# Cross attention and routed experts: sums in their own buffer, the output normalised first, 71 slots

## The chip, the core and the metric

The kernel runs on one core of a Trainium2 chip. The metric is the device time of one execution in microseconds (us). The core has five engines: PE (TensorE, matmuls and transposes), DVE (VectorE), ACT (ScalarE), POOL (GpSimd) and SP (SyncE, whose queue issues most of the DMAs). Each runs its own list of instructions in order and waits on semaphores. Matmuls write into PSUM, of which this kernel uses eight banks: A0 to A3 and B0 to B3.

## What is computed

x is 4096 tokens (16 sequences of 256) of 512 values. The core of the reference:

```python
x = x + xattn(layernorm(x), ctx, ctx, ...)      # 16 heads of 32
#   score = einsum('bshd,bsgd->bshg', Q, K): for one token, its 16 heads against its 16 heads
#   weight = softmax(score); attn = einsum('bshg,bsgd->bshd', weight, V); attn @ Wo.T + bo
x = x + ffn(layernorm(x), ...)
#   logits = z @ gate.T, softmax over 8 experts, the best 2 kept with their weights
#   routed: silu(z @ g) * (z @ u) @ down per picked expert, F = 352
#   shared: the same with 704 hidden values for all tokens
```

Attention is thus within a token, between its heads, and each token goes to two of eight experts.

## The kernel before

**Block loop.** The tokens go through in 16 blocks of 256, two halves of 128 each (SUB = 2). A pass i of the loop (`body(i, ...)`, written out once for each engine) works on three blocks at the same time: scores, softmax and attending of block i; the projections K, Q and V of block i + 1 ("ahead"), with the statistics and the normalising of x of block i + 2 ("ahead2"); and behind them block i - 1 ("behind"): its attended sums are projected by Wo, added to x, normalised to z, and z is transposed, split into two fp16 parts and multiplied with the router's weights. `FULL_PASS` (lines 67 to 78) is PE's order in a pass and says which bank each step fills: X (transposes of the normalised x), S (scores), K, Q, O (projection by Wo), T (transposes of the spread softmax weights), V, Z (transposes of z), L (router logits), P (attend), LT, M0. A step waits until all earlier fills of its bank have been read (`wait_free`); L and Z0 share B2.

**Who does what.** In a pass ACT copies the attended sums out of PSUM (`attended_out`, 24 small copies, DVE does 8 more), then X, K and Q, the exponentials, the T banks (`weights_out`), and the Z banks (`z_out`). DVE reduces the scores, splits operands into a high and a low part, does the softmax, the statistics, `normalise_x`, `add_attended`, `normalise_out`, `values_out`, the largest value of the context block after next (`weigh_context`, `spread_context`), and the low part of z (`z_low`), which is the last reader of a Z bank. POOL spreads the softmax weights into block diagonal form (line 1820, four instructions for each half), finds 1/std (`inverse_std`, lines 1776 and 1777) and splits the context block (`split_context`: a cast, line 1796, and a subtraction, line 373). SP moves K and Q between layouts through 24 DMAs, loads x, the residual and the context, and stores x1, z, the parts of z and the values.

`at_raw`, the buffer of the attended sums, is another view of `z` (line 224). So its writers, ACT and DVE, wait for `z_stored`, the store of the last z to DRAM (lines 1095 and 1414).

**Around it.** Behind the loop an epilogue runs the last block's output between the first steps of the shared experts. Then come the router's ranking, 12 blocks of the shared experts, and the slots: the two picks of each token are sorted by expert into tiles of 128 rows, each tile of one expert. `SLOTS` = 72 of them run (line 34: 64 + 8), in pairs, two buffers each; a slot gathers its 128 rows of z, transposes them, multiplies by gate and up, and by down, and stores 128 rows. Last come the other four blocks of the shared experts together with the weighted sum of each token's two rows.

Of the kernel before, what the change touches and what calls it, by code (L numbers as in the profile page):

```python
# [15 lines left out]
P = 128  # L16
# [5 lines left out]
SUB = 2  # L22
# [11 lines left out]
SLOTS = T * TOPK // P + E  # L34
# [95 lines left out]
def build(nc, x, ctx_t, wq_t, bq, wk_t, bk, wv_t, bv, wo_t, bo, wgate_t, wgu_t, wdn_t, wsgu_t, wsdn_t, out):  # L130
    with ExitStack() as whole:
# [92 lines left out]
        at_raw = z[:, :, :].rearrange("p s (c t) -> p (s c) t", t=BT)  # L224
# [219 lines left out]
        def _(sp):  # L444
# [180 lines left out]
            with sp.Fori(0, SLOTS // 2) as k:  # L625
                for b in range(2):
                    j = k * 2 + b
                    sp.wait_ge(d_out, j + 1)
                    settle(sp)
                    sp.dma_start(y_d[bass.ds(j * P, P), :], y_sb[:, b, :]).then_inc(y_stored[b], 16)  # L630
# [20 lines left out]
        def _(pe):  # L651
# [358 lines left out]
            with pe.Fori(1, SLOTS // 2 - 1) as k:  # L1010
# [6 lines left out]
            j = SLOTS - 2  # L1017
            open_expert(j, 0)
            turn_rows(j + 1, 1, SLOTS // 2 - 1)
            close_expert(j - 1, 1)  # L1020
            turn_act(j, 0)
            open_expert(j + 1, 1)
            close_expert(j, 0)
            turn_act(j + 1, 1)
            close_expert(j + 1, 1)
# [6 lines left out]
        def _(act):  # L1032
# [29 lines left out]

            def z_out(i):
                if not (isinstance(i, int) and i == 1):
                    act.wait_ge(zt_stored, (i - 1) * 16)
                for s in range(SUB):
                    wait_full(act, f"Z{s}", i)
                    turned = bank_ap(f"Z{s}").rearrange("p (c t) -> p c t", c=KC)
                    copy(z_t[:, :, s * P:(s + 1) * P], turned).then_inc(z_turned, 1)
                    nc.scalar.activation(z_parts[:, HI, :, s * P:(s + 1) * P], turned, ACT.Copy, scale=2.0 ** Z_EXP).then_inc(zt_high, 1)  # L1070
# [22 lines left out]
            def attended_out(i):  # L1093
                wait_full(act, "P0", i - 1)
                act.wait_ge(z_stored, i * 16)
# [4 lines left out]
            def body(i, behind, ahead):  # L1100
# [14 lines left out]
                weights_out(1, i)  # L1115
                if isinstance(i, int) and i == NB - 1:
                    act.wait_ge(ws_scaled, 1)
                    shared_high(range(KC))
# [28 lines left out]
            z_out(NB)  # L1147

# [86 lines left out]
            with act.Fori(2, SLOTS // 2 - 1) as k:  # L1235
                for b in range(2):
                    step(k * 2 + b, b, k)
            for j in range(SLOTS - 2, SLOTS):
                step(j, j % 2, j // 2)
            rows_out(SLOTS - 1, 1, SLOTS // 2 - 1)  # L1240
# [29 lines left out]
        def _(dve):  # L1270
# [120 lines left out]
            def z_low(i):  # L1391
                for s in range(SUB):
                    dve.wait_ge(zt_high, (i - 1) * SUB + (s + 1))
# [566 lines left out]
```

## Time and profile before

| | us |
|---|---|
| median of 3 runs | 1666.06 (1652.44 to 1668.23) |
| the profiled execution | 1661.5 |
| its span, first to last instruction | 1659.8 |
| PE busy | 1478.1 (89%) |
| DVE busy | 848.2 (51%) |
| ACT busy | 630.0 (38%) |
| POOL busy | 494.2 (30%) |
| mean granted TensorE clock | 0.954 of full |

The chain of work that ended last consists of PE to 49%, DVE to 15%, SP's queue to 10%, DMA to 8% (5% are the store of z) and ACT to 7%. Busy shares are means over stages: DVE is busy for seven to eight tenths of the block loop (until about 690 us) and for one tenth of the slots (1013 to 1523 us). A row's "idle before" is the time its engine stood still ahead of it, with what ended that.

### The profile page before, as it was taken

What the parts mean: (1) busy time and instruction counts of PE and PEld (TensorE: products, weight loads), DVE (VectorE), ACT (ScalarE), POOL (GpSimd) and SP (SyncE); (2) the same over time, 40 slices, a digit from 0 to 9 for tenths busy, and PEclk for the clock granted to TensorE, in tenths of its full rate; (3) what the DMA queues carried; (4) which work ended last, traced back from release to release, by engine and by line L of the source; (5) the groups of instructions that cost most, each with busy time, mean ns of one, the idle gap of its engine ahead of it and who ended that gap; (6) DMA issues with size and microseconds to landing.
All of it is one profiled execution on the core that took longest, in us unless ns stands there. A gap on an engine that the chain in (4) does not pass through costs nothing.

```text
span 1659.8 us, 32612 instructions
## 1 busy us (share of the span) xinstructions
PE 1478.1 (89%) x10194; PEld 1092.1 (66%) x10211; DVE 848.2 (51%) x1797; ACT 630.0 (38%) x1481; POOL 494.2 (30%) x607
## 2 busy tenths in 40 slices
PE   5489999999999998668979997999999999999786
PEld 5488887788888886446657774666666666666443
DVE  6577788777877887558525532111111111111565
ACT  5255555555555654422114421222222222222111
POOL 4244444433333333102663001111111111111564
PEclk9799999999999998779989998999999999999888
DMA  5346566665665657192344252222222222222897
GB/s 184 78 107 143 144 146 150 155 158 166 158 143 143 143 116 229 56 339 90 52 64 78 76 196 95 76 75 76 75 75 76 74 76 75 76 75 93 283 332 249
DMA packets 258247, 215.61 MB, mean 130 GB/s; under 512 B 182688, under 2 KB 190953, under 8 KB 257850
## 3 DMA queue, kind: packets, MB, share of 16 engines
q1 hardware_dynamic: 240196, 170.63, 37.1%
q0 software_dynamic: 12960, 35.73, 7.6%
q10 hardware_dynamic: 5046, 8.66, 1.6%
q8 instruction: 26, 0.43, 0.1%
q14 instruction: 19, 0.16, 0.0%
HBM read 120.52 MB, written 69.28 MB: 114 GB/s over the span
## 4 chain that ended last, share of the span: by engine, by line
PE 49%; DVE 15%; SPq 10%; DMA 8%; issue 8%; ACT 7%; POOL 1%; another core or an unknown queue 1%; DVEq 0%; ACTq 0%; POOLq 0%
PE psum_a L653 23%; PE psum_b L653 22%; SPq L455 9%; DMA z_rows<-z 5%; ACT z L1034 5%; DVE sc L1364 3%; PE psum_b L961 2%; PE psum_b L983 1%; DMA wgu_in<-expert_rows,pos_ix 1%; DVE d_m L1591 1%; DVE gate_act L1566 1%; DVE k_parts L1307 1%; DVE stats L1292 1%; ACT wgu L1184 1%
## 5 line engine op out<-in xcount | busy, mean ns | idle before, releaser
L653 PE MATMUL psum_a<-wgu,zg_t 128*128 x1728 | 271.4, 314 | 1.7 <-DVE zg_t L1713 1.7
L1718 DVE SCALAR_TENSOR_TENSOR silu<-psum_a,w_scale,silu 128x352 f32<-128x352 f32 x72 | 42.0, 584 | 408.8 <-ACT silu L1217 408.8
L1820 POOL TENSOR_TENSOR spread<-pr,own 128x512 f32<-128x512 f32 x128 | 139.0, 1117 | 357.2 <-DVE pr L1379 352.2
L1894 POOL DMA_INDIRECT zg<-z_rows,gather_ix x72 | 68.1, 946 | 530.5 <-DVE gather_ix L1709 522.8
L653 PEld LDWEIGHTS psum_a<-wgu,zg_t 128*128 128x128 f16 x1728 | 169.6, 98 | 85.5 <-issue 2.4
L653 PE MATMUL psum_b<-wdn,act_t 128*128 (+1 forms) x432 | 197.6, 593 | 0.9 <-ACT act_t L1034 0.9
L653 PE MATMUL psum_b<-wsdn,sh_t 128*128 128x512 f16 (+1 forms) x576 | 150.1, 416 | 43.1 <-DVE sh_t L1572 31.1
L653 PE MATMUL psum_a<-zt_in,wsgu 128*128 128x256 f16 x1536 | 173.5, 275 | 6.0 <-DVE wsgu L1409 5.3
L653 PEld LDWEIGHTS psum_a<-zt_in,wsgu 128*128 128x128 f16 x1536 | 150.5, 99 | 31.5 <-issue 11.6
L653 PEld LDWEIGHTS psum_b<-wsdn,sh_t 128*128 128x128 f16 (+1 forms) x576 | 57.1, 105 | 130.5 <-issue 42.5
L1034 ACT ACTIVATE z<-psum_a 32x128 f32<-32x128 f32 x384 | 102.7, 267 | 54.7 <-DMA z_rows<-z 48.7
L653 PEld LDWEIGHTS psum_b<-wdn,act_t 128*128 128x128 f32 (+1 forms) x432 | 76.6, 191 | 70.0 <-issue 70.0
L1217 ACT ACTIVATE silu<-psum_a,w_scale 128x352 f32<-128x352 f32 x72 | 39.8, 553 | 206.2 <-PE psum_a L653 206.2
L653 PE MATMUL psum_b<-cx_t,wk 128*128 128x256 f32 x768 | 109.2, 298 | 5.6 <-DVE wk L373 5.6
L653 PE MATMUL psum_a<-k_st,q_st 104*128 104x128 f16 x512 | 78.3, 294 | 40.2 <-DMA q_st<-q_parts 24.7
L653 PEld LDWEIGHTS psum_b<-cx_t,wk 128*128 128x128 f32 x768 | 101.7, 203 | 6.1 <-DVE wk L373 6.0
L1161 ACT ACTIVATE gate_act<-psum_a,ws_scale 128x256 f32<-128x256 f32 x64 | 30.0, 471 | 198.5 <-PE psum_a L653 168.5
L653 PE MATMUL psum_b<-xn_t,wq 128*128 128x256 f32 x768 | 104.7, 290 | 0.0
L653 PE MATMUL psum_b<-wo,at_t 128*128 128x512 f32 x384 | 100.5, 416 | 1.1 <-DVE at_t L373 1.1
L1034 ACT ACTIVATE y_sb<-psum_b 128x512 f32<-128x512 f32 x72 | 43.0, 597 | 148.7 <-PE psum_b L653 148.7
L653 PEld LDWEIGHTS psum_b<-xn_t,wq 128*128 128x128 f32 x768 | 97.3, 195 | 0.1
L653 PE MATMUL psum_b<-wv,cx_t 128*128 128x512 f32 x384 | 93.2, 399 | 2.2 <-ACT q_parts L1042 2.2
(229 smaller groups left out, 2385.0 us busy)
## 6 DMA issues: line engine op xcount, KB each, us to landing
expert_rows<-y_sb SPq DMA_DIRECT2D x72, 256.0 KB, 2.9
k_st<-k_parts SPq DMA_DIRECT2D x192, 64.0 KB, 2.1
q_st<-q_parts SPq DMA_DIRECT2D x192, 64.0 KB, 2.2
wgu_in<-in_wgu_t SPq DMA_DIRECT2D x8, 1408.0 KB, 15.6
x_sb<-in_x SPq DMA_DIRECT2D x16, 512.0 KB, 3.5
cx_in<-in_ctx_t SPq DMA_DIRECT2D x16, 512.0 KB, 6.5
x_res<-in_x SPq DMA_DIRECT2D x16, 512.0 KB, 5.2
value_rows<-heads SPq DMA_DIRECT2D x16, 512.0 KB, 6.0
```

Source lines behind the costliest of these rows:

```text
L455: sp.dma_start(dst[HD * n:HD * (n + 1), :, HD * l:HD * (l + 1), :].rearrange("p j m g -> p j (m g)"), parts[HD * l:HD * (l + 1), part].rea ...
L653: return nc.tensor.matmul(o, l, r, start=start, stop=stop)
L961: last = nc.tensor.transpose(t_bank[:, kc * P:(kc + 1) * P], zg[:, b, kc * P:(kc + 1) * P], ident[:, :])
L983: last = nc.tensor.transpose(a_bank[0:fn, f * P:(f + 1) * P], silu[:, b, f0:f0 + fn], ident[:, :])
L1034: return nc.scalar.activation(o, i_, ACT.Copy)
L1161: nc.scalar.activation(gate_act[at:at + fn, f % GB, :], sh_bank(f)[0:fn, 0:BT], ACT.Silu, scale=ws_scale[0:fn, 3:4]).then_inc(silu_ready, 1)
L1184: act.activation(wgu[:, bass.ds(e * UNIT + c * 2 * F, 4 * F)], wgu_in[:, bass.ds(e + 1, 1), c:c + 2, :].rearrange("p o c n -> p (o c n)"), ...
L1217: nc.scalar.activation(silu[:, b, :], psum_a[:, 2 * b * BANK:2 * b * BANK + F], ACT.Silu, scale=w_scale[:, 3:4]).then_inc(g_silu, 1)
L1364: ins = V.tensor_reduce(out=sc[:, s, u * UG:(u + 1) * UG, :], in_=bank_ap(step).rearrange("p (r g t) -> p r g t", r=UG, t=GT), axis=X, op= ...
L1718: V.scalar_tensor_tensor(out=silu[:, b, :], in0=psum_a[:, (2 * b + 1) * BANK:(2 * b + 1) * BANK + F], scalar=w_scale[:, 3:4], in1=silu[:, ...
L1820: G.tensor_tensor(spread[:, u * UG:(u + 1) * UG, :].rearrange("p r (g t) -> p r g t", t=GT), pr[:, s, u * UG:(u + 1) * UG, :].unsqueeze(3) ...
L1894: pool.indirect_dma_start(out=zg[:, b, :], out_offset=None, in_=z_d[:, :], in_offset=bass.IndirectOffsetOnAxis(ap=gather_ix[:, b:b + 1], a ...
```

## The change

It has four parts. The attended sums get a buffer of their own (`at_raw`), and the two waits for `z_stored` move from the copies to DVE's `normalise_out`, the writer of z. On DVE, `normalise_x(i + 2)` and `weigh_context`/`spread_context` move behind `add_attended`, `normalise_out` and `values_out`. The second half of the split of z moves: on ACT `z_high(i, 1)` behind the copies of the second T banks, on DVE `z_low(i, 1)` behind `logits_out`; the wait for `zt_stored` stands at `z_high` now. And `SLOTS` becomes (4096 x 2 + 8 x 127) / 128, rounded down, which is 71, the largest number of tiles that eight experts can need; since it is odd, the first slot of a last pair is run behind the paired loops on each engine (only SP's part of that is shown).

```diff
--- before.py
+++ after.py
@@ -31,7 +31,8 @@
 TOPK = 2
 EPS = 1e-5
 BANK = 512
-SLOTS = T * TOPK // P + E
+SLOTS = (T * TOPK + E * (P - 1)) // P
+PAIRS = SLOTS // 2
 SH_STEPS = 8
 UNIT = 2 * KC * 2 * F
 CONVERT_FROM = 6
@@ -221,7 +222,7 @@
         var_eps = sb("var_eps", [P, 2 * SUB], F32, one)
         rstd = sb("rstd", [P, 2 * SUB], F32, one)
 
-        at_raw = z[:, :, :].rearrange("p s (c t) -> p (s c) t", t=BT)
+        at_raw = sb("at_raw", [P, KC, BT], F32, one)
         ws_rep = xn[:, 0, 0:P]
 
         w_in = [heads[:, :, :, :].rearrange("p h c t -> p (h c t)").rearrange("p (c n) -> p c n", c=KC), spread_t[:, 1].rearrange("p (c n) -> p c n", c=KC),
@@ -622,12 +623,15 @@
             for i in range(converted, SHARED_FIRST):
                 store_base(i, i % 2, i // 2, True)
 
-            with sp.Fori(0, SLOTS // 2) as k:
+            def store_rows(j, b):
+                sp.wait_ge(d_out, j + 1)
+                settle(sp)
+                sp.dma_start(y_d[bass.ds(j * P, P), :], y_sb[:, b, :]).then_inc(y_stored[b], 16)
+
+            with sp.Fori(0, PAIRS) as k:
                 for b in range(2):
-                    j = k * 2 + b
-                    sp.wait_ge(d_out, j + 1)
-                    settle(sp)
-                    sp.dma_start(y_d[bass.ds(j * P, P), :], y_sb[:, b, :]).then_inc(y_stored[b], 16)
+                    store_rows(k * 2 + b, b)
+            store_rows(SLOTS - 1, 0)
 
             def store_out(n, b):
                 sp.wait_ge(c_done, n + 1)
...
@@ -1060,14 +1060,20 @@
                         act.wait_ge(v_stored, (i + 1) * 16)
                 split_heads(f"Q{b}", b, q_whole, q_parts, q_scale[:, 2:3], q_scale[:, 4:4 + KC])
 
+            def turned_out(i, s):
+                wait_full(act, f"Z{s}", i)
+                copy(z_t[:, :, s * P:(s + 1) * P], bank_ap(f"Z{s}").rearrange("p (c t) -> p c t", c=KC)).then_inc(z_turned, 1)
+
+            def z_high(i, s):
+                if s == 0 and not (isinstance(i, int) and i == 1):
+                    act.wait_ge(zt_stored, (i - 1) * 16)
+                nc.scalar.activation(z_parts[:, HI, :, s * P:(s + 1) * P], bank_ap(f"Z{s}").rearrange("p (c t) -> p c t", c=KC),
+                                     ACT.Copy, scale=2.0 ** Z_EXP).then_inc(zt_high, 1)
+
             def z_out(i):
-                if not (isinstance(i, int) and i == 1):
-                    act.wait_ge(zt_stored, (i - 1) * 16)
-                for s in range(SUB):
-                    wait_full(act, f"Z{s}", i)
-                    turned = bank_ap(f"Z{s}").rearrange("p (c t) -> p c t", c=KC)
-                    copy(z_t[:, :, s * P:(s + 1) * P], turned).then_inc(z_turned, 1)
-                    nc.scalar.activation(z_parts[:, HI, :, s * P:(s + 1) * P], turned, ACT.Copy, scale=2.0 ** Z_EXP).then_inc(zt_high, 1)
+                turned_out(i, 0)
+                z_high(i, 0)
+                turned_out(i, 1)
 
             def x_out(i):
 
@@ -1092,7 +1098,6 @@
 
             def attended_out(i):
                 wait_full(act, "P0", i - 1)
-                act.wait_ge(z_stored, i * 16)
                 sums_out(copy, 0, range(4)).then_inc(drained[BANK_OF["P0"]], 1)
                 wait_full(act, "P1", i - 1)
                 sums_out(copy, 1, range(2)).then_inc(half_out, 1)
@@ -1113,6 +1118,8 @@
                 if behind:
                     z_out(i)
                 weights_out(1, i)
+                if behind:
+                    z_high(i, 1)
                 if isinstance(i, int) and i == NB - 1:
                     act.wait_ge(ws_scaled, 1)
                     shared_high(range(KC))
@@ -1145,6 +1152,7 @@
             body(NB - 1, True, False)
             attended_out(NB)
             z_out(NB)
+            z_high(NB, 1)
 
             act.wait_ge(r_shift, 1)
             nc.scalar.activation(d_s[:, :, :], d_s[:, :, :], ACT.Exp).then_inc(r_exp, 1)
...
@@ -1388,12 +1395,11 @@
                 mark(V.tensor_scalar(hidden, power, -1.0, float((2 * 127 + H_EXP - H_ROOM - Z_EXP - W_EXP) << 23), ALU.mult, ALU.add))
                 link(V.tensor_scalar(down, power, float((W_EXP + Z_EXP) << 23), None, ALU.subtract))
 
-            def z_low(i):
-                for s in range(SUB):
-                    dve.wait_ge(zt_high, (i - 1) * SUB + (s + 1))
-                    V.scalar_tensor_tensor(out=z_parts[:, LO, :, s * P:(s + 1) * P], in0=bank_ap(f"Z{s}").rearrange("p (c t) -> p c t", c=KC),
-                                           scalar=2.0 ** Z_EXP, in1=z_parts[:, HI, :, s * P:(s + 1) * P],
-                                           op0=ALU.mult, op1=ALU.subtract).then_inc(drained[BANK_OF[f"Z{s}"]], 1)
+            def z_low(i, s):
+                dve.wait_ge(zt_high, (i - 1) * SUB + (s + 1))
+                V.scalar_tensor_tensor(out=z_parts[:, LO, :, s * P:(s + 1) * P], in0=bank_ap(f"Z{s}").rearrange("p (c t) -> p c t", c=KC),
+                                       scalar=2.0 ** Z_EXP, in1=z_parts[:, HI, :, s * P:(s + 1) * P],
+                                       op0=ALU.mult, op1=ALU.subtract).then_inc(drained[BANK_OF[f"Z{s}"]], 1)
 
             def logits_out(i):
                 wait_full(dve, "L", i)
@@ -1411,7 +1417,6 @@
 
             def attended_out(i):
                 wait_full(dve, "P1", i - 1)
-                dve.wait_ge(z_stored, i * 16)
                 sums_out(V.tensor_copy, 1, range(2, 4)).then_inc(drained[BANK_OF["P1"]], 1)
 
             def split_attended(i):
@@ -1436,6 +1441,7 @@
                     V.bn_aggr(mv[:, SUB + s, :], stats[:, SUB + s, :]).then_inc(stat_ready, 1)
 
             def normalise_out(i):
+                dve.wait_ge(z_stored, i * 16)
                 for s in range(SUB):
                     dve.wait_ge(rstd_ready, stat_no(i, 1, s))
                     V.tensor_scalar(z[:, s, :], x1[:, s, :], mv[:, SUB + s, 0:1], rstd[:, SUB + s:SUB + s + 1], ALU.subtract, ALU.mult).then_inc(z_ready, 1)
@@ -1465,31 +1471,31 @@
                     low_heads(i, "Q0", q_whole, q_parts, q_low)
                     low_heads(i, "Q1", q_whole, q_parts, q_low)
                 softmax(i, 1)
-                if ahead2:
-                    wait_full(dve, "X1", i)
-                    normalise_x(i + 2)
                 if isinstance(i, int) and i == NB - 1:
                     dve.wait_ge(ws_loaded, 48)
                     link(V.tensor_reduce(out=ws_scale[:, 0:1], in_=wsgu_in[:, :, :].rearrange("p c n -> p (c n)"), axis=X, op=ALU.max, apply_absolute_value=True))
                     V.tensor_copy(ws_rep, ws_scale[:, 0:1].broadcast_to([P, P])).then_inc(ws_rep_ready, 1)
                 if behind:
                     add_attended(i)
+                if behind:
+                    normalise_out(i)
+                if ahead:
+                    values_out(i)
                 if ahead2:
+                    wait_full(dve, "X1", i)
+                    normalise_x(i + 2)
                     weigh_context(i + 2)
                 if ahead:
                     spread_context()
                 if behind:
-                    normalise_out(i)
-                if ahead:
-                    values_out(i)
-                if behind:
-                    z_low(i)
+                    z_low(i, 0)
                 if isinstance(i, int) and i == NB - 1:
                     dve.wait_ge(ws_rep_turned, 1)
                     find_scale(ws_scale, psum_b[0][:, 0:P])
                     dve.sem_inc(ws_scaled, 1)
                 if behind:
                     logits_out(i)
+                    z_low(i, 1)
                 if isinstance(i, int) and i == NB - 1:
                     for kc in range(KC):
                         shared_low(kc)
@@ -1546,8 +1552,9 @@
             split_attended(NB)
             add_attended(NB)
             normalise_out(NB)
-            z_low(NB)
+            z_low(NB, 0)
             logits_out(NB)
+            z_low(NB, 1)
             turned_logits_out(NB)
             wait_drained(dve, "LT", NB)
             dve.wait_ge(z_stored, 16 * (NB + 1))
...
```

The order on DVE in the loop, from weigh_context to the second reader of a Z bank, before:

```order
L1318 TENSOR_REDUCE k_scale<-cx_in 128x1 [waits cx_loaded]
L123 REGISTER_ALU
L1322 COPY c_rep<-k_scale 128x128 [waits dve_own]
L1440 ISA
L1441 TENSOR_SCALAR z<-x,mv,rstd 128x512 [waits rstd_ready]
L1440 REGISTER_ALU
L1441 TENSOR_SCALAR z<-x,mv,rstd 128x512 [waits rstd_ready]
L353 REGISTER_ALU
L1313 TENSOR_TENSOR heads<-psum_b,bv_rep 128x512 [waits full_B0]
L1313 TENSOR_TENSOR heads<-psum_b,bv_rep 128x512 [waits full_B1]
L1393 ISA
L1394 SCALAR_TENSOR_TENSOR z_parts<-psum_b,z_parts 128x4x128 [waits zt_high]
```

The same engine from values_out (`heads`) on, now:

```order
L1320 TENSOR_TENSOR heads<-psum_b,bv_rep 128x512 [waits full_B0]
L1320 TENSOR_TENSOR heads<-psum_b,bv_rep 128x512 [waits full_B1]
L354 REGISTER_ALU
L1307 REGISTER_ALU [waits full_B1]
L1308 TENSOR_SCALAR xn<-x_sb,mv,rstd 128x512 [waits rstd_ready]
L1307 REGISTER_ALU
L1308 TENSOR_SCALAR xn<-x_sb,mv,rstd 128x512 [waits rstd_ready]
L1325 TENSOR_REDUCE k_scale<-cx_in 128x1 [waits cx_loaded]
L124 REGISTER_ALU
L1329 COPY c_rep<-k_scale 128x128 [waits dve_own]
L1399 ISA
L1400 SCALAR_TENSOR_TENSOR z_parts<-psum_b,z_parts 128x4x128 [waits zt_high]
```

Two `xn`, the reduction and the copy of the context's largest value now stand between the values and the first `z_parts`, the reader of bank B2; before, nothing did. PE's list at L and the attend step is the same in both (here of before; `z_t,wgate` is L, `spread_t,v_p` the attend step):

```order
L716 REGISTER_ALU [waits drained_B2]
L653 MATMUL psum_b<-z_t,wgate 32x256 [waits z_turned]
L653 MATMUL psum_b<-z_t,wgate 32x256 x3
L359 REGISTER_ALU
L363 REGISTER_ALU [waits drained_A2]
L760 REGISTER_ALU [waits drained_A2,drained_A3,drained_A1,drained_A0]
L653 MATMUL psum_a<-spread_t,v_p 32x128 [waits v_moved]
```

Nothing moved there: L waits for B2's readers before and now.

## Rows read from the trace of the kernel before

**Rows 1.** Waits of PE from 134 to 640 us: us in total, times, longest.
```profile
PE psum_a L653 <- ACT z L1034: 10.9, 23, 2.3
```

**Rows 2.** Timeline of PE, attend steps: start us, us, engine, line, op, out<-in, count, [idle before <- releaser].
```profile
135.89 1.96 PE L653 MATMUL psum_a<-spread_t,v_p 128*32 128x128 f32 x64 [1.55 <-ACT spread_t L1034]
604.89 1.95 PE L653 MATMUL psum_a<-spread_t,v_p 128*32 128x128 f32 x64 [1.01 <-ACT spread_t L1034]
641.70 1.95 PE L653 MATMUL psum_a<-spread_t,v_p 128*32 128x128 f32 x64 [1.55 <-ACT spread_t L1034]
```

**Rows 3.** Chain of waits at 329 us, and ACT's timeline at 336 us.
```profile
329.17 6.89 DMA z_rows<-z
336.08 6.71 ACT L1034 ACTIVATE z<-psum_a 32x128 f32<-32x128 f32 x24 [3.83 <-DMA z_rows<-z]
```

**Rows 4.** Timeline of PE and SP's queue in the pass from 604.89 to 641.70 us.
```profile
629.58 1.91 PE L750 MATMUL psum_a<-ident,spread 128*128 128x128 f32 x16
639.52 0.64 PE L653 MATMUL psum_b<-z_t,wgate 128*32 128x256 f32 x8
628.92 7.77 SPq L455 DMA_DIRECT2D q_st<-q_parts  x12
```

**Rows 5.** Timeline of all engines in the second pass.
```profile
164.16 1.91 PE L750 MATMUL psum_a<-ident,spread 128*128 128x128 f32 x16
164.92 4.39 POOL L1820 TENSOR_TENSOR spread<-pr,own 128x512 f32<-128x512 f32 x4 [0.21 <-PE psum_a L750]
170.19 0.55 DVE L1441 TENSOR_SCALAR z<-x,mv,rstd 128x512 f32<-128x512 f32 x1
171.65 1.28 DVE L1313 TENSOR_TENSOR heads<-psum_b,bv_rep 128x512 f32<-128x512 f32 x2
171.93 1.04 POOL L1796 CAST cx_t<-cx_in 128x1024 fp32r<-128x1024 f32 x1 [0.78 <-PE psum_b L653]
173.05 2.37 POOL L373 TENSOR_TENSOR cx_t<-cx_in,cx_t 128x1024 fp32r<-128x1024 f32 x1
```

**Rows 6.** Timeline: DVE and POOL at 366 us, and at 45 us.
```profile
366.25 1.33 DVE L1441 TENSOR_SCALAR z<-x,mv,rstd 128x512 f32<-128x512 f32 x1
366.27 1.04 POOL L1796 CAST cx_t<-cx_in 128x1024 fp32r<-128x1024 f32 x1 [0.52 <-PE psum_b L653]
44.65 2.66 POOL L373 TENSOR_TENSOR cx_t<-cx_in,cx_t 128x1024 fp32r<-128x1024 f32 x1
45.15 2.71 DVE L1286 SCALAR_TENSOR_TENSOR z<-z_t,ident,z_parts 3x512 f32<-3x512 f32 x1
```

**Rows 7.** Timeline of DVE in a steady pass.
```profile
364.31 1.19 DVE L1318 TENSOR_REDUCE k_scale<-cx_in 128x1 f32<-128x1024 f32 x1
365.65 0.23 DVE L1322 COPY c_rep<-k_scale 128x128 f32<-128x128 f32 x1 [0.15 <-DVE k_scale L1318]
```

**Rows 8.** Timeline of PE, and one stretch: busy us of each engine, granted clock (0.79), DMA.
```profile
101.78 4.62 PE L653 MATMUL psum_b<-cx_t,wk 128*128 128x256 f32 x24
140.12 3.12 PE L653 MATMUL psum_b<-cx_t,wk 128*128 128x256 f32 x24
145.51 0.64 PE L653 MATMUL psum_a<-k_st,q_st 104*128 104x128 f16 x4 [2.27 <-ACT z L1034]
145.90 2.60 PE L653 MATMUL psum_b<-cx_t,wk 128*128 128x256 f32 x12
144.00:148.00 4.00, 2.49 (x15) 2.49 (x16) 1.98 (x9) 3.81 (x15) 0.00 (x0) 0.79 0.47 59
```

**Rows 9.** Chain of waits in the slots: first gate_up counted and the 66th behind it.
```profile
1041.33 3.58 PE psum_a L653 x24
...
1498.43 3.58 PE psum_a L653 x24
```

**Rows 10.** Timeline of DVE in the epilogue.
```profile
712.06 0.69 DVE L1394 SCALAR_TENSOR_TENSOR z_parts<-psum_b,z_parts 128x512 f16<-128x512 f32 x1 [0.29 <-ACT z_parts L1070]
713.56 0.42 DVE L1400 COPY logits_t<-psum_b 128x256 f32<-128x256 f32 x1 [0.81 <-PE psum_b L653]
```

More of the change, by code:

```diff
@@ L1009, in _ @@
             turn_act(1, 1)
-            with pe.Fori(1, SLOTS // 2 - 1) as k:
+            with pe.Fori(1, PAIRS) as k:
                 for b in range(2):
@@ L1016, in _ @@
                     turn_act(j, b)
-            j = SLOTS - 2
+            j = SLOTS - 1
             open_expert(j, 0)
-            turn_rows(j + 1, 1, SLOTS // 2 - 1)
             close_expert(j - 1, 1)
             turn_act(j, 0)
-            open_expert(j + 1, 1)
             close_expert(j, 0)
-            turn_act(j + 1, 1)
-            close_expert(j + 1, 1)
             pe.wait_ge(d_out, SLOTS)
@@ L1234, in _ @@
                 step(j, j % 2, j // 2)
-            with act.Fori(2, SLOTS // 2 - 1) as k:
+            with act.Fori(2, PAIRS) as k:
                 for b in range(2):
                     step(k * 2 + b, b, k)
-            for j in range(SLOTS - 2, SLOTS):
-                step(j, j % 2, j // 2)
-            rows_out(SLOTS - 1, 1, SLOTS // 2 - 1)
+            step(SLOTS - 1, 0, PAIRS)
+            rows_out(SLOTS - 1, 0, PAIRS)
             def load_base(n):
@@ L1727, in _ @@
                 rows_low(j + 1, 1 - j)
-            with dve.Fori(1, SLOTS // 2 - 1) as k:
+            with dve.Fori(1, PAIRS - 1) as k:
                 for b in range(2):
@@ L1733, in _ @@
                     rows_low(j + 1, 1 - b)
-            gated(SLOTS - 2, 0)
-            rows_low(SLOTS - 1, 1)
-            gated(SLOTS - 1, 1)
+            j = SLOTS - 3
+            index_out(j + 2, 0, PAIRS)
+            gated(j, 0)
+            rows_low(j + 1, 1)
+            gated(j + 1, 1)
+            rows_low(j + 2, 0)
+            gated(j + 2, 0)
             def combine(n, b, k):
@@ L1898, in _ @@
             gather(1, 1)
-            with pool.Fori(1, SLOTS // 2) as k:
+            with pool.Fori(1, PAIRS) as k:
                 for b in range(2):
                     gather(k * 2 + b, b)
+            gather(SLOTS - 1, 0)
             for b in range(2):
-                pool.wait_ge(y_stored[b], 16 * (SLOTS // 2))
+                pool.wait_ge(y_stored[b], 16 * ((SLOTS + 1 - b) // 2))
             def fetch(n, b):
```

## The prediction

> **What bounds the kernel now.** I read the chain of waits first, then PE's waits, then one pass of the block loop on each engine. The kernel has two long stages that the change touches: the loop over 16 blocks of 256 tokens (95 to 690 us of the span) and the expert slots (1013 to 1523 us).
>
> In the block loop I measure pass i from the attend step (PE, spread_t by v_p) of block i - 1 to that of block i: passes 2 to 13 take (604.89 - 135.89) / 12 = 39.1 us, pass 14 only 36.8 us [rows 2]. PE is busy for nine tenths of it, yet it is not the limit: ACT stands still for 3.83 us before it copies the attended sums, because they go into `z`, and the rows of z of the block before are still being read by their DMA [rows 3]. That wait makes PE's own waits on ACT's copies, 10.9 us over the loop in 23 places [rows 1]. Pass 14, in which SP has no x to load and the store has landed in time, shows the loop without the wait: PE reaches the first weight transposes (T0) 24.69 us after its attend, L (z_t by wgate, the router's logits) 9.94 us after T0, and the next attend 12.12 us after T0 [rows 2, 4]. In the slots PE repeats a period of (1498.43 - 1041.33) / 66 = 6.93 us with no gap that another engine fills [rows 9].
>
> **The change, part by part.** I number times in a pass from T0's start.
>
> *Own buffer for the sums.* ACT and DVE no longer wait for z_stored before the copies. The wait moves to DVE's normalise_out, 30 us later in the pass, where the store has long landed (it takes 6.9 us [rows 3]); it costs nothing there. Attend to T0 then takes 24.69 us in each pass, as in pass 14. DVE comes earlier too up to the softmax, but PE's T0, not DVE, releases POOL's second spread (0.76 after T0 [rows 5]), so what counts is PE.
>
> *The x rows of block i+2 normalised behind the output.* DVE now runs: add_attended, normalise_out, values_out, normalise_x, weigh_context, spread_context, first z_low, logits_out, second z_low. Ahead of the output there is now nothing to do while POOL spreads and then finds rstd, so the output is not earlier than POOL allows: z from 6.03, values at 7.49 [rows 5]; that is a pass in which POOL was the limit already. PE goes on from V to Z and the second weight transposes without a wait: it would be at L at 9.94.
>
> L, however, writes the PSUM bank that holds Z0 and waits until the first z_low has read it. Before, that z_low stood right behind values_out and was done in time. Now normalise_x, weigh_context and spread_context stand between. Their cost:
> - Values end at 8.7. The first xn starts there, while POOL's cast of the context (7.77, 1.04 long) runs; POOL's subtraction, 2.37 us, is due at 8.89 [rows 5].
> - In the trace such an instruction does not run beside POOL. The second z, of the same form as xn, takes 1.33 us instead of 0.55 [rows 5, 6] and ends 0.27 after POOL's cast. And at 45.15 a DVE instruction of 3 x 512 with two inputs in SBUF takes 2.71 us and ends 0.55 after a subtraction of POOL of the same shape as here [rows 6]. There the one that waited went first and POOL's next one after it.
> - So: first xn through at 9.1 (0.27 behind the cast), the subtraction from 9.1 to 11.5, the second xn at 11.75.
> - weigh_context and its wait 1.34, spread_context 0.15 until the next can start [rows 7]: 13.25. First z_low 0.69 [rows 10]: 13.95.
> L starts at 14.0 instead of 9.94, and attend 0.64 behind it, at 14.6 (ACT has drained the transposes by 11.6). A pass is 24.69 + 14.6 = 39.3 us.
>
> The Trainium skill, "SBUF — State Buffer", section "Who interferes with whom", says that a tensor_scalar in its two-port mode and a GpSimd instruction exclude each other for a whole instruction, first come first served. By it the subtraction is paid in full, and the sum stays as it is; without it, it would be the first rival's.
>
> *The clock.* PE now stands still for 4.0 us in one piece in every pass, where it had several waits of up to 1.0. A wait of 2.27 us was followed by a granted clock of 0.79 over four microseconds, that is a part of it at 1.2 instead of 2.4 GHz, and by 12 matmuls that took 2.60 us, where 24 such take 3.12; another wait was followed by 24 that took 4.62 [rows 8]. What this costs after L is not in the trace: nothing, if the slow part lies in the wait itself; at most the 1.5 us of the second row; nearest is a slow stretch over L, the attend steps and the transposes of x, which are short and not all bound by the clock. I take 0.7 a pass.
>
> The Trainium skill, "TensorE: Matmul & The Clock Gate", section "HAM oscillation — how this bites in real kernels", tells of a loop with one wait a turn that pays for the lower clock in every turn. By it this term is paid 13 times, as I take it; without it the sum below would be 9 us less.
>
> *ACT.* z_high of the second half moves behind the transposes' copies, which start 0.5 us earlier. In passes 1 to 13 L hides that; pass 14 (no x ahead) gets 0.5. *SP.* Its load of x waits for normalise_x, and x_res, x1 and z are issued behind it. SP is through with the queries 31.8 us after the attend in pass 14 [rows 2, 4]; xn is ready at 24.69 + 11.75 = 36.4. So these four issues come up to 4.6 us later. Nothing waits for them before the middle of the next pass, and with some 2.7 us for the four SP is still ahead of its next wait, the second z_low, now about 1 us into the next pass. The values' store behind that comes 3 us later in the pass, and with it the 16 reads of values, the keys and the queries in one row: the queries end at 34 instead of 31.8, and the next scores stand behind the next attend, at over 41. It costs nothing.
>
> *Around the loop.* Block 0 waits for the queries' DMA anyway. In the last block ACT's copies come earlier (by less than the 3.83 of rows 3, as other waits lie beside it) and ws_scale is found one z_low, 0.69, earlier. In the epilogue the second z_low, which started at 712.06, comes behind logits_out, which ends at 713.98 [rows 10]: 1.9 us later, and the column store, the router and POOL's lists wait for it. I set these against each other: 0, between -2 and +2.
>
> *71 slots.* One period less, -6.9. The odd slot's code does the same per slot.
>
> **Sum**, against the profiled execution (1661.5 us, span 1659.8):
> passes 2 to 13: 12 x 39.3 = 471.6 instead of 604.89 - 135.89 = 469.0 [rows 2]: +2.6. Pass 1, which had no wait for the store: L 4.1 later, less the 1.55 wait that stood behind it [rows 2]: +2.5. Clock 13 x 0.7: +9.1. Pass 14: -0.5. Slots: -6.9. Total +6.8, **1668 us**. The median shown, 1666.1, is 4.6 above the profiled execution and the runs spread from 1652 to 1668; I do not add the difference, since of the three runs one lies 9 below the profiled execution and two 5 and 7 above. About 1%, 17 us, is what a measurement of this kernel can tell from no change.
>
> **The likeliest case** (62%): DVE's chain behind the values holds L, as worked out. Clock 0 to 1.2 a pass and 0.2 either way in each pass: 1657 to 1677, "within 1%".
>
> **Rivals.**
> 1. *The second xn is not held* (16%). If DVE takes both xn before POOL's subtraction, or the subtraction starts late, z_low ends 1.95 us earlier and a pass is 37.4: 13 x 1.95 = 25 less, 1643 (1634 to 1650), faster. For it: in the pass of rows 5 both z go in 0.55, since POOL has nothing long at hand. Against it: at both places of rows 6 where POOL had, the later instruction was held to its end, and here POOL's longest is due 0.2 after the first xn starts.
> 2. *The clock costs more than the wait removed* (15%), the case on the other side. If the slow stretch begins only at the keys' projections, or lasts through two such stretches, it costs 1.5 to 2 us in each pass: 1679 to 1685, slower by over 1%. It decides from 1.45 a pass on. For it: in both rows the slow matmuls are the projections behind the wait. Against: at 145.90 the projection stood half a microsecond behind the wait; here L and the attend steps, 0.64 and 1.95 long, stand between.
> 3. *DVE keeps up and PE is the limit* (5%): the pass is 24.69 + 12.12 - 0.5 = 36.3, 12 x 36.3 - 469 = -33, with the rest 1620. It would need the first z_low at 9.9, 3 us before the three steps ahead of it can be done; nothing speaks for it.
> 2% are left for what I have not seen, on the slow side.
>
> **Numbers.** Range 1630 to 1682: it leaves out the third rival, the end of the second and the low end of the first. Faster by over 1% 0.20, within 1% 0.61, slower by over 1% 0.19.
>
> **What would show it.** Right: ACT's copies start with the attend and wait for no DMA; PE's largest wait in a pass is at L, 4 us, released by DVE's z_parts; the second xn takes 2.4 us or more; POOL's second spread starts 0.76 behind T0; passes of 39 to 40.5; 71 slots at 6.93. A granted clock below 1.0 in each pass shows the clock's term. Wrong: xn pairs of 1.1 us, a wait at L of 2 us or none, passes of 36 to 37.5; or slow projections in each pass and passes above 40.8.

## The result, and the profile after

The changed kernel takes **1684.7 us** in the median of four runs (1681.9 to 1685.8), the kernel before beside it 1664.1 (four runs, 1652.4 to 1668.2): a ratio of **1.0133 with a 95% interval of 1.0079 to 1.0186**. In a second set of runs, on another chip, it was 1.0193 (1.0142 to 1.0243). It is slower by 1.3%; the forecast was 1668 us with a range up to 1682, "within 1%". The result lies 2.7 us above the range, among the times of the second rival.

The profiled execution took 1685.75 us, span 1684.0, against 1661.5 and 1659.8 before: 24.2 us more. This is where it lies, by the same events of PE in both traces (us; minus is less time):

| stretch | before | after | difference | forecast |
|---|---|---|---|---|
| start to the attend step of block 0 | 95.2 | 95.2 | 0 | 0 |
| pass 1 | 40.7 | 43.3 | +2.6 | +2.5 |
| passes 2 to 13 | 469.0 | 491.7 | +22.7 | +2.6, clock +8.4 |
| pass 14 | 36.8 | 37.9 | +1.1 | -0.5, clock +0.7 |
| last pass, to L of the epilogue | 71.2 | 69.1 | -2.1 | 0 |
| to the first slot (shared expert) | 304.2 | 312.3 | +8.1 | 0 |
| slots | 502.6 | 496.5 | -6.1 | -6.9 |
| behind the slots | 140.2 | 138.1 | -2.1 | 0 |

PE's waits from 134 to 690 us, after (us in total, times, longest). The row that was the loop's wait before [rows 1] is reduced to two waits; a new one stands in each of passes 1 to 13. Two more rows of the kernel before, from 134 to 640 us, are as good as gone: 14.1 us in 13 waits for ACT's spread_t at the attend step, and 13.1 us in 22 waits for DVE's z.

```profile
PE psum_b L657 <- DVE z_parts L1400: 49.3, 13, 3.8
PE psum_a L657 <- ACT at_raw L1034: 3.8, 2, 2.1
PE psum_b L657 <- DVE at_t L374: 1.1, 1, 1.1
PE psum_a L657 <- ACT spread_t L1034: 1.1, 1, 1.1
```

One steady pass after (pass 6), DVE and then POOL (start us, us, engine, line, op, out<-in, count, [idle before <- releaser]). T0 of this pass is at 328.97.

```profile
334.77 0.55 DVE L1447 TENSOR_SCALAR z<-x,mv,rstd 128x512 f32<-128x512 f32 x1 [2.74 <-POOL rstd L1788]
335.77 0.55 DVE L1447 TENSOR_SCALAR z<-x,mv,rstd 128x512 f32<-128x512 f32 x1 [0.46 <-POOL rstd L1788]
336.23 1.28 DVE L1320 TENSOR_TENSOR heads<-psum_b,bv_rep 128x512 f32<-128x512 f32 x2
337.43 3.12 DVE L1308 TENSOR_SCALAR xn<-x_sb,mv,rstd 128x512 f32<-128x512 f32 x2
340.47 1.21 DVE L1325 TENSOR_REDUCE k_scale<-cx_in 128x1 f32<-128x1024 f32 x1
341.83 0.23 DVE L1329 COPY c_rep<-k_scale 128x128 f32<-128x128 f32 x1 [0.15 <-DVE k_scale L1325]
341.97 0.68 DVE L1400 SCALAR_TENSOR_TENSOR z_parts<-psum_b,z_parts 128x512 f16<-128x512 f32 x1
343.49 0.43 DVE L1406 COPY logits_t<-psum_b 128x256 f32<-128x256 f32 x1 [0.84 <-PE psum_b L657]
```

```profile
336.73 1.04 POOL L1807 CAST cx_t<-cx_in 128x1024 fp32r<-128x1024 f32 x1 [1.00 <-PE psum_b L657]
337.86 2.41 POOL L374 TENSOR_TENSOR cx_t<-cx_in,cx_t 128x1024 fp32r<-128x1024 f32 x1
```

The two xn take 3.12 us together and end at 340.55, 0.28 behind the end of POOL's subtraction; the first z_low ends at 342.65. PE in the same pass:

```profile
342.79 0.64 PE L657 MATMUL psum_b<-z_t,wgate 128*32 128x256 f32 x8 [3.79 <-DVE z_parts L1400]
343.34 2.85 PE L657 MATMUL psum_a<-spread_t,v_p 128*32 128x128 f32 x64
346.12 1.02 PE L657 MATMUL psum_b<-strip_sum,logits_t 128*128 128x8 f32 x4
347.00 0.45 PE L785 MATMUL psum_b<-ident,c_rep 128*128 128x128 f32 x1
347.73 1.89 PE L683 MATMUL psum_b<-ident,xn 128*128 128x128 f32 x8
```

L starts at T0 + 13.82. Behind it the attend step takes 2.85 us, where it took 1.95 before [rows 2]. The stretches there (busy us of PE, PEld, DVE, ACT, POOL, then the granted clock, DMA share, GB/s) show when the clock is low:

```profile
338.00:342.00 4.00, 1.00 (x10) 0.76 (x7) 3.85 (x5) 2.88 (x6) 2.27 (x1) 1.00 0.01 4
342.00:346.00 4.00, 3.21 (x72) 2.57 (x72) 1.68 (x4) 1.41 (x6) 0.00 (x0) 0.78 0.89 265
346.00:350.00 4.00, 4.00 (x26) 3.75 (x23) 2.25 (x9) 3.83 (x15) 0.00 (x0) 0.50 1.05 412
350.00:354.00 4.00, 4.00 (x31) 3.94 (x31) 3.75 (x13) 2.60 (x8) 0.00 (x0) 0.87 0.72 246
```

PE stands still at full clock; once it works again the clock falls, for four microseconds to 0.50, that is 1.2 GHz throughout. So it is at 12 of the 13 waits; at the first the fall comes inside the wait (0.83 from 132.5 to 137.9 us, and L itself took 1.08 instead of 0.64). The price has two sizes. In eight of passes 2 to 13 the granted clock is 0.84 over the 10.6 us from L on, and the pass takes 40.6 or 40.7 us; in four it is 0.68 to 0.77, and the pass takes 41.2 to 41.8. The fall shown is one of the four. ACT's copies wait for PE alone, and no DMA stands in their row any more, where [rows 3] had 3.83 us:

```profile
344.53 6.71 ACT L1034 ACTIVATE at_raw<-psum_a 32x128 f32<-32x128 f32 x24 [3.65 <-PE psum_a L657]
```

The slots, in the chain of waits after (start us, us, what): a period of 6.92 us, as in [rows 9].

```profile
1074.53 3.58 PE psum_a L657 x24
1078.11 0.44 PE psum_b L965 x4
1078.54 2.58 PE psum_b L657 x6
1081.12 0.33 PE psum_b L987 x3
1081.45 3.58 PE psum_a L657 x24
```

Two questions are left by the traces: whether the low clock, and not some other hindrance of the attend step, makes the 1.7 us by which a pass (40.97) exceeds the 39.3 worked out without the clock; and whether the 8.1 us in the shared expert's stage, where PE waits 16.1 us for `base<-x_rows`, belong to the change.

### The profile page after: what moved, and what is told of

It reads as the page before. It is cut to its first block, busy times and chain, and to the rows that moved or that the text cites. A ratio compares the mean times of both kernels' runs of the same rounds, so it can differ in the third digit from the quotient of the medians.

```text
span 1684.0 us, 32459 instructions
## 1 busy us (share of the span) xinstructions
PE 1487.9 (88%) x10157; PEld 1111.2 (66%) x10174; DVE 858.8 (51%) x1794; ACT 628.8 (37%) x1476; POOL 496.3 (29%) x606
## 4 chain that ended last, share of the span: by engine, by line
PE 68%; DVE 12%; DMA 6%; issue 5%; POOL 4%; ACT 2%; SPq 2%; another core or an unknown queue 0%; DVEq 0%; POOLq 0%; ACTq 0%
PE psum_b L657 36%; PE psum_a L657 27%; DVE xn L1308 2%; POOL spread L1831 2%; DMA base<-x_rows 2%; PE psum_b L965 2%; SPq L456 2%; PE psum_b L987 1%; DMA base_rows<-base 1%; DMA wgu_in<-expert_rows,pos_ix 1%; PE psum_b L683 1%; DVE k_scale L1325 1%; DMA out_rows<-wgu_in 1%; DVE heads L1320 1%; PE psum_a L754 1%
## 5 line engine op out<-in xcount | busy, mean ns | idle before, releaser
L657 PE MATMUL psum_a<-zt_in,wsgu 128*128 128x256 f16 x1536 | 176.9, 278 | 22.6 <-DMA base<-x_rows 16.1
L657 PEld LDWEIGHTS psum_b<-wsdn,sh_t 128*128 128x128 f16 (+1 forms) x576 | 56.3, 103 | 117.4 <-DVE sh_t L1579 39.3
L1034 ACT ACTIVATE at_raw<-psum_a 32x128 f32<-32x128 f32 x384 | 103.0, 268 | 60.4 <-PE psum_a L657 55.9
L657 PEld LDWEIGHTS psum_b<-wdn,act_t 128*128 128x128 f32 (+1 forms) x426 | 75.6, 191 | 69.1 <-issue 69.0
```

What stands on the lines that cost most here:

```text
L657: return nc.tensor.matmul(o, l, r, start=start, stop=stop)
L1034: return nc.scalar.activation(o, i_, ACT.Copy)
```

## The experiments

The pass times below are the mean of passes 2 to 13 from a profiled execution, attend to attend; within one kernel passes 2 to 13 agree to 0.1 us where the clock stays full and nobody waits for the store. The ratio is that to the kernel before, run beside it on the same chip.

**The wait filled.** Transposes of the identity matrix, read by nobody, where PE stood still:

```diff
                 transpose_weights(1, i)
+                if behind and ahead:
+                    wait_drained(pe, "V0", i)
+                    for _ in range(30):
+                        nc.tensor.transpose(psum_b[0][:, 0:P], ident[:, :], ident[:, :])
                 if behind:
                     route(i)
```

> The changed kernel, with 30 more PE transposes of the identity matrix between the second weight transposes and L in passes 1 to 14 that have blocks on both sides; they take about 3.6 us and lie inside PE's 3.8 us wait at L, so that PE works where it stood still; their result is read by nobody. My theory (the lower granted clock behind the wait costs 1.9 us a pass): attend after L returns from 2.85 us or more to 1.95, passes 2 to 13 fall from 40.97 to 39.0 to 39.3 us, no low clock in the loop, total about 25 us less than the changed kernel, 1658 to 1664 us. Rival (the steps behind L are slow for another reason, operands that ACT or DVE still write, or a port): passes stay at 41 us and the total at 1683 to 1687, or above it by whatever the transposes overrun. As predicted (0.7 a pass): 9 us less, 1675.

Measured: passes of **39.05 us** instead of 40.97, 1646.5 us in the median of ten runs, ratio 0.9967 (0.9938 to 0.9995). PE of this kernel, with T0 at 318.18:

```profile
328.02 3.44 PE L828 MATMUL psum_b<-ident 128*128 128x128 f32 x30
332.00 0.64 PE L657 MATMUL psum_b<-z_t,wgate 128*32 128x256 f32 x8 [0.53 <-DVE z_parts L1404]
332.52 1.95 PE L657 MATMUL psum_a<-spread_t,v_p 128*32 128x128 f32 x64
334.40 0.61 PE L657 MATMUL psum_b<-strip_sum,logits_t 128*128 128x8 f32 x4
```

L starts at T0 + 13.82 as without the fill, to a hundredth; DVE holds it as long. Yet the attend step is back at 1.95 us and the loop has no low clock. So 1.92 us a pass are the clock's: more work on PE made the kernel faster. The rival, operands or a port, falls. The changed kernel without any fill shows the same once (second execution, below): in its pass 12 the clock stayed at 1.00 behind a wait of 3.79 us, the attend step took 1.95 us and the pass 39.34.

The totals of this kernel and of the three that ran beside it (the subtraction held, the three steps back, the first z_low ahead) lie below what was expected of them, while their passes came out as expected. The expected totals started from the 1684.7 us of the first chip; the kernel before ran at 1653.6 beside these four, 10.5 less than there, and in their profiled executions the stage between the loop and the slots took 293.8 to 301.8 us instead of 312.3.

**The fill shortened**, to 8 and to 16 transposes, each measured once.

> The fill of 30 transposes cut to 8 (0.9 us), at the start of PE's wait at L: 2.9 us of standing still are left in each pass, and L starts at T0 + 13.8 as before. Asked: does the price of the low clock shrink with the wait or is it paid whole? If whole: passes 2 to 13 at 41.0 us, the clock below 1 once in each pass. If in proportion to the wait: 39.05 + 1.9 x 2.9 / 3.8 = 40.5. If only a wait of more than 2.9 us lowers the clock: 39.05.

> The same with 16 transposes (1.85 us): 1.9 us of standing still are left, less than the 2.27 us behind which the kernel before showed a lower clock once, more than the 1.7 us of the kernel with the subtraction held, which showed none. If the price is paid whole: passes at 41.0. If in proportion: 39.05 + 0.95 = 40.0. If a wait of 1.9 us lowers nothing: 39.05, no low clock in the loop.

The same L and attend with 8, and then with 16:

```profile
340.68 0.64 PE L657 MATMUL psum_b<-z_t,wgate 128*32 128x256 f32 x8 [2.93 <-DVE z_parts L1404]
341.20 3.61 PE L657 MATMUL psum_a<-spread_t,v_p 128*32 128x128 f32 x64
```

```profile
338.59 0.64 PE L657 MATMUL psum_b<-z_t,wgate 128*32 128x256 f32 x8 [2.06 <-DVE z_parts L1404]
339.11 2.94 PE L657 MATMUL psum_a<-spread_t,v_p 128*32 128x128 f32 x64
```

Passes of 40.83 us with a wait of 2.93 us, and of 40.71 with 2.06 (of it, pass 2 took 39.37 and the others 40.3 to 41.8). L starts at T0 + 13.8 in all of them, so the difference from 39.05 is the clock's price alone: 1.8 and 1.7 us in the mean, against 1.9 for a wait of 3.79 and nothing for one of 0.53. Pass by pass the price is the same in all three kernels: mostly 1.6 us (granted clock 0.84 over the 10.6 us from L on), now and then 2.1 to 2.8 (0.68 to 0.77). The means differ because the longer kind came four times with the whole wait and twice with each of the shorter ones, and because one wait of 2.06 us, in pass 1, was followed by full clock. So was the last wait of 2.93 us, in pass 13, and pass 14 behind it took 36.32 us instead of 37.88. A price is thus paid behind nearly every wait, not behind each, and a quarter or a half of the wait taken away buys almost nothing. Of the answers expected "paid whole" was right, if 41.0 us is read as 40.8 and 40.7. The totals, one run each, were 1683.3 and 1667.0 us beside 1667.8 for the kernel before; 15 of the 16 us between the two lie in the stage between loop and slots (312.8 and 298.0), not in the loop.

**The subtraction held.** POOL waits for c_rep of the block before it starts the cast and the subtraction:

```diff
                 if ahead2:
+                    pool.wait_ge(c_rep_ready, i + 2)
                     split_context(i + 2)
```

> The changed kernel, with POOL's subtraction of the context of block i+2 held until DVE has written c_rep of that block, so that it does not start while DVE normalises x. If the subtraction holds the second xn: the xn pair falls from 3.1 to about 1.1 us, L starts about T0 + 11.8 instead of 13.8, PE's wait there is 1.8 instead of 3.8 us, and a pass is 24.69 + 11.8 + 0.55 = 37.0 us without a clock loss, total 1684.7 - 13 x 3.9 = 1634; with the clock loss of 1.9 still paid in each pass 1659. Rival (the xn pair is slow because of something else, its own form or the bank): pair 3.1, total 1683 to 1687.

Measured: passes of **36.91 us**, 1614.1 us, ratio 0.9746 (0.9702 to 0.979). DVE, and then PE, with T0 at 307.26:

```profile
315.72 0.99 DVE L1308 TENSOR_SCALAR xn<-x_sb,mv,rstd 128x512 f32<-128x512 f32 x2
316.63 1.21 DVE L1325 TENSOR_REDUCE k_scale<-cx_in 128x1 f32<-128x1024 f32 x1
318.14 0.68 DVE L1400 SCALAR_TENSOR_TENSOR z_parts<-psum_b,z_parts 128x512 f16<-128x512 f32 x1
```

```profile
318.95 0.64 PE L657 MATMUL psum_b<-z_t,wgate 128*32 128x256 f32 x8 [1.66 <-DVE z_parts L1400]
319.50 1.96 PE L657 MATMUL psum_a<-spread_t,v_p 128*32 128x128 f32 x64
```

The xn pair falls from 3.12 to 0.99 us, L starts at T0 + 11.69, and the wait of 1.66 us that is left brings no low clock in any of the 13 passes. The hold is shown: the subtraction beside it cost DVE 2.1 us, and through the clock PE another 1.9. POOL's two instructions start 3.6 us later in the pass (T0 + 11.38 instead of 7.76), and nobody waits for them.

**The three steps back ahead of the output** (own buffer, split z_low and 71 slots stay):

```diff
                 softmax(i, 1)
+                if ahead2:
+                    wait_full(dve, "X1", i)
+                    normalise_x(i + 2)
...
                     add_attended(i)
+                if ahead2:
+                    weigh_context(i + 2)
+                if ahead:
+                    spread_context()
                 if behind:
                     normalise_out(i)
                 if ahead:
                     values_out(i)
-                if ahead2:
-                    wait_full(dve, "X1", i)
-                    normalise_x(i + 2)
-                    weigh_context(i + 2)
-                if ahead:
-                    spread_context()
                 if behind:
                     z_low(i, 0)
```

> The changed kernel with the three steps of block i+2 (normalise_x, weigh_context, spread_context) back where they were, ahead of the output; own buffer for the sums, split z_low and 71 slots stay. My theory (the order alone holds L and the own buffer is worth its wait): no wait of PE at L, L at about T0 + 10, passes 2 to 13 at 36.3 to 36.9 us as pass 14 had before, total 1684.7 - 13 x 4.4 = 1627 us, between 1622 and 1634. Rival (the wait for the store was hidden anyway, another wait takes its place, as of DVE's output for Z): passes 38 to 39, total 1650 to 1660.

Measured: passes of **36.34 us**, 1607.4 us, ratio **0.9715 (0.9667 to 0.9763)**, the fastest kernel of this study and a version that beats both the kernel before and the changed one. L waits for nobody (it starts at T0 + 9.94); what is left is one wait for ACT at the attend step:

```profile
349.97 0.64 PE L657 MATMUL psum_b<-z_t,wgate 128*32 128x256 f32 x8
351.67 1.95 PE L657 MATMUL psum_a<-spread_t,v_p 128*32 128x128 f32 x64 [1.06 <-ACT spread_t L1034]
```

**The first z_low ahead of normalise_x:**

```diff
+                if behind:
+                    z_low(i, 0)
                 if ahead2:
                     wait_full(dve, "X1", i)
                     normalise_x(i + 2)
                     weigh_context(i + 2)
                 if ahead:
                     spread_context()
-                if behind:
-                    z_low(i, 0)
```

> The changed kernel with the first z_low moved ahead of normalise_x; all else stays. My theory: z_low ends at about T0 + 10.5, L is not held, the xn pair still 2.4 us or more, so that the logits' transposes wait up to 1 us for DVE behind weigh_context; passes 2 to 13 at 36.5 to 37.3 us, total 1627 to 1638 us. Rival (the three steps that stand behind it now only move the wait to the next step that waits for DVE, the transposed logits, LT, or the keys): a wait of 3 us or more there, passes 39 to 41, total 1658 to 1685.

Measured: passes of 37.15 us, 1622.3 us, ratio 0.9797 (0.9754 to 0.9839). L waits for nobody. The xn pair still takes 2.39 us, and PE waits up to 0.4 us in each pass for DVE's copy of the logits. Against the kernel with the steps back all of the 0.8 us lie between the attend step and the keys' projection (5.01 us instead of 4.22). So the x steps may stand behind the output at a cost of 0.8 us a pass, if only the one short step that frees L's bank is not behind them.

**The own buffer alone**, put into the kernel before:

```diff
-        at_raw = z[:, :, :].rearrange("p s (c t) -> p (s c) t", t=BT)
+        at_raw = sb("at_raw", [P, KC, BT], F32, one)
...
-                act.wait_ge(z_stored, i * 16)
...
-                dve.wait_ge(z_stored, i * 16)
...
             def normalise_out(i):
+                dve.wait_ge(z_stored, i * 16)
```

> The kernel before, with the own buffer for the attended sums and the wait for the rows' store moved to DVE's output; order of the steps and 72 slots as before. My theory: no wait of ACT for the store, passes 2 to 13 fall from 39.1 to 36.3 to 36.9 us, total 12 x 2.5 = 30 us less than the kernel before, 1620 to 1632. Rival (the gain needs the split z_low and z_high too, or another wait takes its place): passes of 38 or more, less than 15 us gained.

Measured: passes of **36.83 us**, 1638.7 us, 26.8 less than the kernel before beside it, ratio 0.9815 (0.9769 to 0.986). The gain was expected at 30 us. PE's waits for ACT's copies of the sums are gone, and those for DVE's z too; what is left in passes 2 to 13 is 1.6 us at the attend step each time, behind ACT's second z_high. The kernel with the steps back (36.34) has the split z_high and z_low as well, and waits 1.06 us there, so that split is worth 0.49 a pass.

**The buffer shared again**, in the changed kernel (the same four lines the other way).

> The changed kernel with the attended sums kept in z again, and ACT's and DVE's waits for the rows' store ahead of the copies, as before; the order of the steps and 71 slots stay. My theory (the two parts of the change are separate, and the later x makes the store later): the store, issued at attend - 0.6 us and 6.2 us long, holds ACT's copies by about 4.4 us; passes 2 to 13 at 43 to 45 us, total 1684.7 + 12 x 2 to 4 = 1709 to 1733. Rival (both waits overlap, so that the own buffer brought nothing in this order): passes of 41, total 1681 to 1688.

Measured: passes of 43.17 us, 1715.3 us, ratio 1.0316 (1.0268 to 1.0365). ACT's and PE's waits both stand (the row shows the first 14 of ACT's 24 copies):

```profile
358.34 3.92 ACT L1034 ACTIVATE z<-psum_a 32x128 f32<-32x128 f32 x14 [9.13 <-DMA z_rows<-z]
```

The own buffer brings 2.20 us a pass in the new order and 2.25 in the old: its effect and that of the order add up.

**71 slots alone**, in the kernel before (the hunks of the diff that name SLOTS or PAIRS, and nothing else).

> The kernel before with 71 instead of 72 slots and nothing else. Expected: one period of 6.93 us less, passes of the block loop unchanged at 39.1, total 7 us less than the kernel before, ratio 0.9958. Rival (the last, odd slot exposes a chain that the pair hid, or the gathers of the slots were the limit): 0 to 3 us less, or slower.

Measured: 1664.6 against 1665.5 us, ratio 0.9984 (0.9955 to 1.0013), which holds both the expected 0.9958 and no change at all. The stage itself is clearer: from the first to the last slot 496.2 us, in every kernel with 71 slots 495.1 to 496.7, and 502.6 and 503.0 in the two with 72. The slot is gone in full; the total cannot show it, for the reason that the next run gives.

**The changed kernel again.**

> The changed kernel once more, unaltered, beside the kernel before, for what the fill cannot tell: whether PE's wait for the base rows' DMA behind the block loop (16.1 us in the changed kernel, none in the kernel before, 2.0 to 8.2 in four variants) belongs to the change or varies from run to run. The block loop should repeat (passes 2 to 13 of 41.0 us). If the wait belongs to the change: 14 to 18 us again. If it varies: any other value, 0 to 9 us, and the total falls by as much of it as is not hidden, up to 8 us.

Measured: 1693.3 us (1672.8 to 1702.0), ratio 1.0193 (1.0142 to 1.0243); passes of 40.76, the wait at L again 49.3 us over 13 times, of which the one in pass 11 brought no low clock (pass 12: 39.34 us). In the profiled execution PE waited 1.7 us for `base<-x_rows` where the first had 16.1, and from L of the epilogue to the first slot it took 303.6 us, before 304.2. So the change does not always bring the 8.1 us of the first comparison. More is not shown: the profiled execution was the fastest of the four (1672.8 us; the others 1690 to 1702), and the medians here differ by 27.8 us, of which the loop and the slot, by the profiled executions, account for about 14. Whether the changed kernel has this stage long more often stays open. That stage took 293.8 to 316.5 us in eleven of the profiled executions and 334.0 in the one of the own buffer alone (30 us more than in the kernel before, in an execution that lies 23 us above this kernel's median), with waits now on a DMA, now on DVE, now on no releaser that the profile names. What sets it I have not settled.

## Why the prediction was wrong

**Own buffer.** Right. ACT waits for no DMA in the loop. From attend to T0 it is 24.71 us where the clock stays full (the kernel with the fill, 293.47 to 318.18), forecast 24.69. By itself the buffer is worth 2.25 us a pass.

**DVE's order and the wait at L.** Right in every step of the chain. Forecast: first z_low through at T0 + 13.95, L at 14.0, attend 0.64 behind. Measured: 13.68, 13.82 and 0.55. The second xn was held as read from [rows 6]: forecast end 11.75, measured 11.58. Without the clock the pass would have been 39.05 us (the fill), forecast 39.3. One reading beside it was off: the kernel before had single waits of up to 1.55 us at the attend step (in [rows 2] too) and one of 2.3, not "up to 1.0". The first rival (xn not held) needed an xn pair of 1.1 us and did not come; the run with the subtraction held is that rival made real, and its pass is 36.91, forecast 37.4. The third rival's pass, 36.3, is the one of the kernel with the steps back, 36.34.

The Trainium skill, "SBUF — State Buffer", section "Who interferes with whom", has DVE's two-port tensor_scalar and a GpSimd instruction exclude each other for a whole instruction; the 3.12 and 0.99 us of the xn pair agree.

**The clock.** This is the step that failed: its mechanism was right, its **size** was not. I took 0.7 us a pass from between 0 and 1.5 and called the upper end unlikely, because L and the attend step are short and "not all bound by the clock". They are: the attend step's 64 small matmuls grew from 1.95 to 2.85 us (in other passes up to 3.65), the logits' from 0.61 to 1.02, the transposes of x from 1.05 to 1.89. The pass lost 1.92 us, 23 us over passes 2 to 13 and about 1.5 in pass 14, instead of 9 in all. The miss of 1.22 us, 13 times, is 15.9 us. The most that I allowed, 1.5 us, is a little less than what the mildest of these passes pay (1.6); the four with the lower clock pay 2.1 to 2.8, so the second rival's "two such stretches" were there too. The two profiled executions differ by 16.1 us without the 8.1 of the shared expert's stage, forecast 6.8: 6.8 + 15.9, less 3.0 for a pass that was 0.25 shorter than worked out and less 3.6 for the smaller terms below.

The two parts of my argument against the second rival are what misled. From [rows 8] I priced only the projections, which I had slow rows of, and averaged the unknown work behind L to half. And I took the slow part to lie partly inside the wait itself, where at 12 of the 13 waits the stretches show full clock throughout the wait and the fall behind it.

The Trainium skill, "TensorE: Matmul & The Clock Gate", section "HAM oscillation — how this bites in real kernels", has a loop with one wait a turn pay in every turn. The trace agrees, 13 waits and a low clock at each; in the second execution it was 12 of 13.

**ACT.** The 0.5 us were there in every pass that L does not hold (36.83 against 36.34). In pass 14 the low clock behind the last wait at L covered them: +1.1 instead of -0.5.

**Around the loop and slots.** Forecast 0, between -2 and +2. The last pass took 38.1 instead of 40.2 us, and from its attend step to L of the epilogue 31.0 in both. Slots -6.9 forecast, -6.1 measured between these two executions, 6.9 by the means of all. Whether the +8.1 of the shared expert's stage is any part of the change is open, as said above, and the -2.1 behind the slots may be none either: that stretch took 137.5 to 141.5 us over the kernels of this study.

In one line, per pass: 39.08 before; own buffer 36.83; with the split z_high and z_low 36.34; with the x steps moved 39.05 (as the kernel with the fill shows it); with the clock 40.97.

## What to carry to other kernels

Price a new wait of the matmul engine as the wait plus a surcharge of the clock for each time it comes (here mostly 1.6 us, at times 2.1 to 2.8, behind waits of 2.1 to 3.8 us, none behind 1.7), and price that from all the work behind it, small matmuls included, not from the one row that happens to be slow in the trace. A step that only frees a PSUM bank belongs ahead of any long chain on its engine, and a chain moved next to another engine's long instruction may be held for the whole of it. When a wait cannot be removed, useless work may still pay, if it fills nearly all of it: here 30 transposes brought 1.9 us a pass, 16 of them 0.3.

## What the hardware showed that I had not expected

- The price of the low clock hardly shrinks with the wait: in the mean 1.9, 1.8 and 1.7 us a pass behind waits of 3.79, 2.93 and 2.06 us, and none behind 1.66 (in the kernel with the subtraction held) and 0.53.
- A wait at L of 2.06 us or more had three prices: mostly 1.6 us, now and then 2.1 to 2.8, and at three of 52 waits (the changed kernel twice, the fills of 8 and 16) nothing.
- 3.4 us of transposes that nobody reads made each pass 1.9 us shorter.
- The same kernel's shared-expert stage took 312.3 us in one execution and 303.6 in another, and the medians of the kernel before were 1664.1, 1653.6 and 1665.5 us in three sets of runs. Gains of 7 us, as of the slot, are seen in the stage and not in the total.
